# One projection moved a place in the table of units, and VectorE's leftover unit put ahead of its first maxima

## The reference

```python
qkv = X @ W_qkv + b_qkv                       # X: normalised, scaled and shifted x
qkv = qkv.reshape(b, l, H, 3 * DK).transpose(0, 2, 1, 3)
Q, K, V = jnp.split(qkv, 3, axis=-1)
scores = jnp.einsum('bhqd,bhkd->bhqk', Q, K) / np.sqrt(DK).astype(np.float32)
attn = jax.nn.softmax(scores, axis=-1)
out = jnp.einsum('bhqk,bhkv->bhqv', attn, V)
out = out.transpose(0, 2, 1, 3).reshape(b, l, H * DK)
return out @ W_fc + b_fc
```

## Time and profile before

| what | value |
|---|---|
| time, median of 3 runs | 1769.37 us (1760.49 to 1769.71) |
| the profiled execution's own time | 1768.75 us |
| its span, first to last instruction | 1767.0 us |
| PE busy | 1631.5 us, 92% |
| POOL busy | 1211.2 us, 69% |
| DVE busy | 1134.6 us, 64% |
| ACT busy | 829.0 us, 47% |
| granted TensorE clock, mean over the span | 0.968 |

### The profile page before, as it was taken

How to read it: one execution, slowest core, us unless ns; L and a number is a source line. 1 busy time by engine, 2 the same in 40 slices (tenths; PEclk the granted TensorE clock), 3 DMA queues, 4 the chain that set the end, 5 groups by cost and what they waited for, 6 DMA issues and landing times. The chain is left out here.

```text
span 1767.0 us, 31100 instructions
## 1 busy us (share of the span) xinstructions
PE 1631.5 (92%) x10443; PEld 934.7 (53%) x10443; DVE 1134.6 (64%) x1919; ACT 829.0 (47%) x1176; POOL 1211.2 (69%) x584
## 2 busy tenths in 40 slices
PE   4799999999999999999999999999999999756996
PEld 3454555555555555555555555555555555344886
DVE  5677666666666666666666666666666665387887
ACT  3354444444444444444444444444444444236874
POOL 3287777778777777777777787787777778520134
PEclk8799999999999999999999999999999999767999
DMA  2000000000000000000000000000000000300010
GB/s 91 17 25 31 31 31 30 30 30 30 30 26 24 28 30 30 30 30 30 30 30 30 22 26 30 30 30 26 28 30 30 30 26 15 90 0 25 31 36 30
DMA packets 66883, 54.15 MB, mean 31 GB/s; under 512 B 4734, under 2 KB 61083, under 8 KB 66843
## 3 DMA queue, kind: packets, MB, share of 16 engines
q1 hardware_dynamic: 66688, 53.63, 9.3%
q10 hardware_dynamic: 154, 0.03, 0.0%
HBM read 31.35 MB, written 2.36 MB: 19 GB/s over the span
## 5 line engine op out<-in xcount | busy, mean ns | idle before, releaser
L547 POOL TENSOR_TENSOR ACC<-ACC,PR 128x1024 f32<-128x1024 f32 x382 | 912.2, 2388 | 191.1 <-ACT PR L614 169.2
L644 DVE TENSOR_REDUCE NMH<-ps_mx 128x2 f32<-128x1024 f32 x508 | 618.3, 1217 | 498.1 <-PE ps_mx L816 498.1
L614 ACT ACTIVATE PR<-ps_s 128x1024 f32<-128x1024 f32 x512 | 498.1, 1024 | 439.2 <-PE ps_s L837 436.3
L847 PE MATMUL ps_o<-PR,V 128*64 128x512 f32 x2048 | 496.0, 605 | 0.0
L547 POOL TENSOR_TENSOR ACC<-PR 128x1024 f32<-128x1024 f32 x64 | 151.1, 2361 | 153.6 <-ACT PR L614 153.6
L847 PEld LDWEIGHTS ps_o<-PR,V 128*64 128x64 f32 x2048 | 124.2, 136 | 247.4 <-issue 177.9
L816 PE MATMUL ps_mx<-KH,QH 64*128 64x512 f32 x1016 | 232.3, 450 | 8.0 <-DVE NMH L644 8.0
L831 PE MATMUL ps_s<-QH,KH 64*128 64x512 f32 x1024 | 204.9, 394 | 0.0
L833 PE MATMUL ps_s<-QL,KH 64*128 64x512 f32 x1024 | 204.3, 393 | 0.0
L835 PE MATMUL ps_s<-QH,KL 64*128 64x512 f32 x1024 | 204.0, 391 | 0.0
L837 PE MATMUL ps_s<-NR,onesr 64*128 64x512 f32 x1024 | 203.4, 389 | 0.0
(11 more groups left out here) (208 smaller groups left out, 1739.5 us busy)
## 6 DMA issues: line engine op xcount, KB each, us to landing
hcur<-hT SPq DMA_DIRECT2D x32, 512.0 KB, 3.0
R<-rs_dram SPq DMA_DIRECT2D x128, 128.0 KB, 3.0
Wraw<-in_L_attn_W_qkv SPq DMA_DIRECT2D x32, 192.0 KB, 2.4
x<-in_L_attn_X SPq DMA_DIRECT2D x4, 512.0 KB, 5.2
Wfc<-in_L_attn_W_fc SPq DMA_DIRECT2D x32, 64.0 KB, 2.3
hT<-in_L_attn_X SPq DMA_DIRECT2D x4, 512.0 KB, 6.3
out<-e_res SPq DMA_DIRECT2D x7, 256.0 KB, 2.3
e_hTs<-hT_hi SPq DMA_DIRECT2D x6, 256.0 KB, 2.3
```

The costliest lines, as they stand in the source:

```text
L547: G.tensor_tensor(ACC[:, ch, :, :], a, PR[:, t, :, :], ALU.add).then_inc(added, 1)
L614: A.activation(PR[:, t, :, :], ps_s[:, s % 2, :, :], ACT.Exp, scale=SCALE).then_inc(exp_done, 1)
L644: D.tensor_reduce(NMH[:, ch, kc, :, i], banks[:, :, :], AX, ALU.max, negate=True).then_inc(mx_red, 1)
L847: last = T.matmul(ps_o[half(h), :], V[:, u, t, half(h)], PR[:, t, h, :], start=(t == 0), stop=(t == 7))
```

## The change

Two things change. In the table the fc unit of chunk 0 goes from place (3, 0) to (3, 1), the first v unit from (3, 1) to (4, 1), and the second v unit from (4, 1) to (5, 0). The units' order among themselves stays. And VectorE does its part of the unit of place (j - 1, 1) before it reduces the first maxima of group j, where it did so after. Line numbers behind line 708 are one lower in the changed kernel.

```diff
         UNITS = {(0, 0): ("k", 1, 0), (0, 1): ("k", 1, 1), (1, 1): ("q", 1, 0), (2, 1): ("rs", 0, 1),
-                 (3, 0): ("fc", -1, 0), (3, 1): ("v", 1, 0), (4, 1): ("v", 1, 1), (5, 1): ("q", 1, 1),
+                 (3, 1): ("fc", -1, 0), (4, 1): ("v", 1, 0), (5, 0): ("v", 1, 1), (5, 1): ("q", 1, 1),
                  (6, 1): ("rs", 1, 0), (7, 1): ("fc", -1, 1)}
...
             def pair(n, u):
                 for j in range(8):
-                    maxima(n, 2 * j)
-
                     if j > 0:
                         unit_here(n, u, (j - 1, 1))
                     elif has(n - 1):
                         unit_here(n - 1, 1 - u, (7, 1))
+                    maxima(n, 2 * j)
                     maxima(n, 2 * j + 1)
                     unit_here(n, u, (j, 0))
```

## The result

| | before | changed |
|---|---|---|
| time, median (lowest to highest) | 1767.8 us (1760.49 to 1769.71) | 1845.28 us (1841.31 to 1848.05) |
| the profiled execution's own time | 1768.75 us | 1846.48 us |
| its span | 1767.0 us | 1844.7 us |
| mean granted TensorE clock | 0.968 | 0.969 |

The ratio is 1.0445, with a 95% interval of 1.0408 to 1.0482: slower, by 77.7 us between the two profiled executions. 1855 was predicted, with a range of 1828 to 1895.

What follows compares the result with a forecast made beforehand. TensorE's instruction list was taken to bound the attention stage. Holes adding 119 us (154 of them) less gains of 33 us gave net +86 us on 1768.75, so 1855 us, with a range of 1828 to 1895.

Steps and rivals of the forecast that it cites:

- k, q: Places (0, 1), (1, 1), (5, 1): reduction waits until ScalarE's KL is done; 93 TensorE holes of 0.71 us, 66 us added.
- rs: Places (2, 1) and (6, 1): reduction comes late behind NR and RS; holes of 0.87 us, 26 and 27 us added.
- fc, group 4: Place (3, 1): reduction behind fc's add just in time, costing nothing; if 0.1 late, 12 us over both fc places.
- fc, group 0: Place (7, 1): reduction behind fc's add just in time, costing nothing; if 0.1 late, 12 us over both fc places.
- wait in front of fc, group 3: fc of chunk 0 goes behind PV and its reciprocal comes earlier, so its 30 waits, 28.5 us, go.
- wait in front of k, group 0: Place (0, 0): k waits for fc's add; the earlier add saves 0.15 us in some 30 pairs, 4.5 us.
- NR at T + 0.20: Place (2, 1): NR starts 0.20 us after T, the group's first maxima start on TensorE; bounds T + 0.04 and T + 0.30.
- The 0.10 us behind each hole: After delayed second maxima PV starts 0.43 us behind them, not 0.33; without this the forecast is 15 us less.
- The rival in which GpSimd blocks Wlo longer: Place (6, 1): Wlo waits for GpSimd's next add, 76 us more, 1931 us; chance 0.18 for Wlo as before or worse.
- both reasons that I gave: Group 7's T comes later against GpSimd's add blocking Wlo: 0.71 us by q's hole, 1.1 by group 5's v unit.
- faster: VectorE finishes every unit in time, no reduction is late and only the 33 us gains stay: 1736 us; chance 0.03.
- no change: Holes sum to just the gains, 33 us, from rs or the k and q units alone; chance 0.03.

## Why the prediction was right

**The mechanism.** It went as forecast. RS no longer holds fc up, VectorE's unit delays the first reduction, the reduction's end holds the second maxima, and the hole moves everything behind it. Each step has its row above, and taking it away by kind or covering it gave the time back.

**The terms.** I took, from both timelines, the distance from first to second maxima and from there to the next matmul in all 251 groups, and averaged by the unit in front. The columns show these means, before and after:

| unit in front, number | to the second maxima | from there on | effect | predicted |
|---|---|---|---|---|
| k, q: 93 | 2.19, 2.78 | 0.33, 0.43 | +63 us | +66 |
| rs: 61 | 2.24, 2.88 | 0.35 without the wait of fc, 0.43 | +44 us | +53 |
| fc, group 4: 30 | 2.18, 2.17 | 0.33, 0.40 | +2 us | 0 |
| fc, group 0: 31 | 2.18, 2.21 | | +1 us | 0 |
| wait in front of fc, group 3: 30 | | 1.35, 0.33 without its hole | -31 us | -28.5 |
| wait in front of k, group 0: 31 | | 0.46, 0.39 | -2 us | -4.5 |

They sum to +77 us, against 77.7 measured and 86 predicted. The largest miss is rs, and less by the start of NR than by two other sizes. I had NR at T + 0.20; it starts at T + 0.18 on average in group 3 (T + 0.23 in the pair above) and at T + 0.14 in group 7, where T = 689.15:

```profile
689.15 0.50 PE L815 MATMUL ps_mx<-KH,QH 64*128 64x512 f32 x2
```

```profile
690.76 1.16 DVE L644 TENSOR_REDUCE NMH<-ps_mx 128x2 f32<-128x1024 f32 x1
```

That reduction is at T + 1.61, and the one of group 3 at T + 1.66 on average, against T + 1.66 predicted. But from its start to the second maxima it is 1.22 us (666.77 to 667.99), not the 1.27 that I took from the earlier trace rows for all kinds: the reduction behind RS takes 1.16 us, the one there 1.21. (The late reduction of the earlier trace rows is the first of group 3, not of group 2; the argument is the same.) And without a hole the second maxima stood at T + 2.18 to 2.19 on average in the loop and not at T + 2.16, which makes each hole less of a loss, those of k and q too.

Three small terms were off. Of the 0.15 us in front of k that I put down to fc's add, 0.06 stayed when the add came earlier (0.39 against 0.33). The reduction behind fc starts at T + 0.88 in group 4, but in group 0 at T + 0.82 and T + 0.99 in turn from pair to pair, so that every other one comes late: 1 us in all. And PV follows the second maxima of group 4 after 0.40 us.

The 0.10 us behind each hole, read from a single event of the second pair, came out right 154 times. No row had explained it, so that was luck. It need not be a price of waiting: in group 4, where no idle time stands before the second maxima, 0.07 of it are there too (673.52 to 673.92).

**Wlo.** The rival in which GpSimd blocks Wlo longer did not come. Two Wlo on VectorE in group 6 of the changed kernel, and NR behind them:

```profile
687.92 0.69 DVE L636 TENSOR_TENSOR Wlo<-Wraw,Whi 128x128 fp32r<-128x128 f32 x2
689.29 0.69 DVE L664 TENSOR_TENSOR NR<-ps_w,mask 128x512 fp32r<-128x512 f32 x1 [0.68 <-PE ps_w L780]
```

GpSimd at that time:

```profile
685.90 4.95 POOL L547 TENSOR_TENSOR ACC<-ACC,PR 128x1024 f32<-128x1024 f32 x2 [0.28 <-ACT PR L614]
```

They take 0.69 us here, 2.18 before, and are done at 688.61, 0.68 us before NR starts. The experiments show both reasons that I gave, apart. The longest Wlo of the whole run in the changed kernel, with the table alone, and with the order alone:

```profile
L636 DVE TENSOR_TENSOR Wlo<-Wraw,Whi x64: 276/283/519, 41.9 to 1510.0; 128x128 fp32r<-128x128 f32 x64
```

```profile
L636 DVE TENSOR_TENSOR Wlo<-Wraw,Whi x64: 277/284/1216, 42.9 to 1405.5; 128x128 fp32r<-128x128 f32 x64
```

```profile
L636 DVE TENSOR_TENSOR Wlo<-Wraw,Whi x64: 276/284/1384, 42.6 to 1511.8; 128x128 fp32r<-128x128 f32 x64
```

Against 2052 ns before, the new table with its v unit in group 5 takes 0.84 us off, the new order with its hole of q 0.67, and both 1.53. It is as if Wlo's end were nailed to the end of the add: it starts at 687.92, when the first of the two adds from 685.90 (4.95 / 2 = 2.48 us each) is nearly through, and the second Wlo ends at 688.61, just behind that add's end at 688.38. The first Wlo of a pair ends 0.15 to 0.16 us behind the end of the add that it meets, in every pair of the loop and in all nine traces, whether it starts 0.46 us behind that add's start or 2.03. That agrees with the exclusive lock that the Trainium skill describes ("SBUF — State Buffer", section "SBUF: two separate sides"). The rival was not far off: Wlo starts 2.02 us behind the start of an add of 2.48, 0.46 us before the next one. No run had Wlo start closer than 0.46 us behind the start of an add, so the full price that I gave to the rival was not seen.

**The other two rivals.** In *faster* no reduction was to start later than T + 0.89; of those behind a unit only the ones behind fc keep that (T + 0.88 in group 4, T + 0.82 in every other pair in group 0), with k and q at T + 1.50. In *no change* one kind of hole was to be missing; both are there.

## What to carry to other kernels

Where two engines hand one buffer back and forth, what an engine does first is to be judged by how late the other may get the buffer back, not by the order in which the work arrived: here the reduction had 0.35 us to spare (T + 0.54 to T + 0.89), and a unit of 0.7 to 1.5 us went in front of it. When a change has two parts, ask whether both take away the same wait: here either did, one for nothing and one at a price of some 110 us. And a waiting matmul can be covered by moving it down its own list, but that move has its own price, which a control without the wait shows.

## What the runs showed that I had not expected

Splitting PV around the maxima costs 0.34 us in the group shown, although no engine waits: PV starts 0.10 us later behind scores than the maxima do (687.34 to 689.60 is 2.26 us, where the maxima start after 2.16 in the earlier trace rows), two PV halves take 1.01 us each until the next matmul where the whole takes 1.87, and PV starts 0.42 us behind the maxima, not 0.33. Over 94 splits it was 32 us by the times and 30 by the traces. What causes it, and what causes the 0.10 us behind each hole, no run here shows.
